# Attention scores of a two-layer kernel in tiles of four heads by 32 queries, over only the keys up to them

## The reference, cut to what matters

```python
q = (x @ Wq).reshape(B, S, 16, 192)            # 128 without, 64 with rotation
k = concat([k_nope, broadcast(k_rope)])        # k_nope, v from a 64-wide latent
scores = einsum('bqhd,bkhd->bhqk', q, k) / sqrt(192)
scores = where(tril(ones((S, S))), scores, finfo.min)
attn = softmax(scores, axis=-1)
out = einsum('bhqk,bkhd->bqhd', attn, v).reshape(B, S, 16 * 128) @ Wo
```

## Time and profile before

| | |
|---|---|
| time, median of 3 runs | 873.41 us (871.42 to 873.88) |
| profiled execution | 871.95 us, span of its instructions 870.2 us |
| PE busy | 831.8 us (96%) |
| DVE, ACT, POOL busy | 715.8 (82%), 543.4 (62%), 478.7 us (55%) |
| mean granted PE clock | 0.988 |

### The profile page before, as it was taken

The page is one execution under the profiler, slowest core; times in us unless marked ns, Lnnn a source line. Parts: engine busy times, 40 slices in busy tenths (PEclk is TensorE's granted clock), DMA queues, the critical chain, the costliest instruction groups (busy, mean ns, idle before and its releaser), DMA issues.

```text
span 870.2 us, 22877 instructions
## 1 busy us (share of the span) xinstructions
PE 831.8 (96%) x7736; PEld 759.5 (87%) x7736; DVE 715.8 (82%) x2467; ACT 543.4 (62%) x1611; POOL 478.7 (55%) x1245
## 2 busy tenths in 40 slices
PE   4989999999998789999999999999999999999996
PEld 3978999888897779999999999999999999999975
DVE  6898787898685768988889898898988989888874
ACT  5544444444655747677676676766777677786672
POOL 7832012113134655767657677575766757676653
PEclk9989999999999989999999999999999999999999
DMA  8510110000001111111111112121121111212110
GB/s 299 208 32 1 61 61 2 1 1 1 1 28 43 34 37 46 42 49 35 52 38 51 46 37 55 34 54 45 37 55 31 51 48 41 51 33 54 47 32 20
DMA packets 56277, 41.21 MB, mean 47 GB/s; under 512 B 30304, under 2 KB 53216, under 8 KB 55520
## 3 DMA queue, kind: packets, MB, share of 16 engines
q1 hardware_dynamic: 55968, 39.62, 16.2%
q10 hardware_dynamic: 192, 0.13, 0.1%
HBM read 14.53 MB, written 4.19 MB: 22 GB/s over the span
## 4 chain that ended last, share of the span: by engine, by line
PE 79%; SPq 7%; DVE 4%; POOL 4%; issue 3%; DMA 1%; ACT 1%; POOLq 0%; DVEq 0%; ACTq 0%
PE bank L472 49%; PE bank L660 16%; PE bank L686 8%; SPq L437 5%; SPq L368 3%; PE bank L534 2%; POOL par L1686 1%; PE bank L625 1%; PE bank L544 1%; DVE PT L1494 1%; DVE SM L1474 1%; DMA QT<-qa 1%; POOL G L1686 1%; PE bank L584 1%; PE bank L487 1%
## 5 line engine op out<-in xcount | busy, mean ns | idle before, releaser
L950 ACT ACTIVATE SM<-SM,stb 128x256 f32<-128x256 f32 (+1 forms) x512 | 226.5, 444 | 88.0 <-DVE stb L1474 87.1
L1858 POOL TENSOR_SCALAR SM<-SM,stb 128x256 f32<-128x256 f32 (+1 forms) x512 | 210.9, 430 | 117.3 <-DVE stb L1482 112.9
L660 PE MATMUL bank<-KT,QT 128*128 128x256 f32 (+1 forms) x1024 | 197.2, 333 | 10.4 <-DMA QT<-qa 5.2
L660 PEld LDWEIGHTS bank<-KT,QT 128*128 128x128 f32 x1024 | 150.1, 192 | 32.3 <-DVE stb L1474 10.4
L1474 DVE CUSTOM_DVE_ANT_0 SM<-bank,CONST 128x256 f32<-128x256 f32 (+1 forms) x512 | 154.7, 348 | 17.4 <-PE bank L660 16.0
L472 PE MATMUL bank<-yh,wq_lo 128*128 128x256 f32 x512 | 158.3, 309 | 0.0
L472 PE MATMUL bank<-yl,wq_hi 128*128 128x256 f32 x512 | 145.7, 285 | 0.0
L472 PE MATMUL bank<-yh,wq_hi 128*128 128x256 f32 x512 | 145.6, 284 | 0.0
L1494 DVE STREAM_TRANSPOSE PT<-SM 128x512 f32<-128x512 f32 x192 | 134.7, 702 | 9.0 <-PE bank L686 8.8
L472 PEld LDWEIGHTS bank<-yh,wq_lo 128*128 128x128 f32 x512 | 98.3, 192 | 1.6
L472 PEld LDWEIGHTS bank<-yl,wq_hi 128*128 128x128 f32 x512 | 98.1, 192 | 1.6
(11 more groups left out here) (204 smaller groups left out, 1957.0 us busy)
## 6 DMA issues: line engine op xcount, KB each, us to landing
QT<-qa SPq DMA_DIRECT2D x508, 32.0 KB, 1.9
C<-KV SPq DMA_DIRECT2D x256, 16.0 KB, 1.8
out<-fo SPq DMA_DIRECT2D x32, 128.0 KB, 1.8
X<-in_x SPq DMA_DIRECT2D x7, 512.0 KB, 11.1
stage<-in_wqn SPq DMA_DIRECT2D x2, 1024.0 KB, 9.6
stage<-in_wo SPq DMA_DIRECT2D x2, 1024.0 KB, 5.1
stage<-in_w1t SPq DMA_DIRECT2D x4, 256.0 KB, 5.5
stage<-in_w2t SPq DMA_DIRECT2D x2, 512.0 KB, 7.2
```

Of the source, the lines that this page charges most:

```text
L660: i = e.matmul(sbank[n % 2][:, nk * j:nk * j + nk], Q[:, h % 8, 128 * qt:128 * qt + 128], KT[b % 3][:, h % 2, 0:nk], start=True, stop=True)
L950: i = e.activation(M[:, nk * j:nk * j + nk], M[:, nk * j:nk * j + nk], ACT.Exp, bias=S[:, 0, j:j + 1], scale=-1.0, accum_out=S[:, 1, j:j + 1])
L1858: i = e.tensor_scalar(P[:, nk * j:nk * j + nk], P[:, nk * j:nk * j + nk], S[:, 2, j:j + 1], 1.0, ALU.mult, ALU.mult)
```

## The change

A unit of scores becomes a set of tiles of four heads by 32 queries, each over only the 32(q+1) keys up to the end of its query block q (0 to 7). There are ten units a batch, in a new order: for each half of the heads, two units of the blocks 6 and 7, two of the blocks 4, 5, 0, 1, one of the blocks 2 and 3 of both sets of four heads. The stationary operand holds 32 queries of four heads. To take it as one row of 128 equally spaced words, each head's queries are stored in QT and qa by place in block: token 32n + i at word 8i + n. So it is read with a step of eight words, and `queries` and `turn_queries` write with a step of eight words. `turn_queries` is two instructions instead of one. `most`, `exps` and `normalise` have widths of 32(q+1). `turn_weights` has two instructions in the units of four tiles. In `l1_pv` all heads' products of a query block skip the key blocks past it, so their width is 256, 192, 128 or 64. POOL clears the five SM buffers once after layer 0 (`clean`). Tokens are in natural order, so the reversals in `scan` and in POOL's tables go. All tables and lags were made anew for ten units, and some steps of layer 0 moved by one or two; with them units of scores stand behind `l1_pv` and `l1_q` of the same step instead of ahead of them.

```diff
-ORDER = (3, 0, 2, 1, 5, 4)
-UNITS = 12
+ORDER = (2, 3, 0, 4, 1, 7, 8, 9, 5, 6)
+UNITS = 10
-LAG_T, LAG_V, LAG_L = 4, 5, 6
-LAG_O, LAG_R, LAG_C = (8, 9), (8, 9), (9, 10)
+LAG_T, LAG_V, LAG_L = 4, 6, 6
+LAG_O, LAG_R, LAG_C = (7, 7), (8, 8), (9, 11)
-Q_AT = {2: (1, 0), 5: (3, 2), 9: (7,), 10: (5,), 11: (6, 4)}
+Q_AT = {0: (0,), 2: (1,), 3: (3,), 4: (2,), 6: (7, 5), 9: (6, 4)}
...
 def unit(n):
...
+    b, (h, k) = n // UNITS, divmod(ORDER[n % UNITS], 5)
+    if k < 2:
+        return b, h, [(k, 6, 0), (k, 7, 256)]
+    if k < 4:
+        return b, h, [(k - 2, 4, 0), (k - 2, 5, 192), (k - 2, 0, 384), (k - 2, 1, 448)]
+    return b, h, [(0, 2, 0), (0, 3, 128), (1, 2, 256), (1, 3, 384)]
+def tiles(n):
+    return [(p, q, slice(at, at + 32 * q + 32)) for p, q, at in unit(n)[2]]
...
+        def by_place(t):
+            return t.rearrange("p h (q n) -> p h n q", n=8)
...
             def l1_s(n):
...
-                for j, h in enumerate(hd):
-                    i = e.matmul(sbank[n % 2][:, nk * j:nk * j + nk], Q[:, h % 8, 128 * qt:128 * qt + 128],
-                                 KT[b % 3][:, h % 2, 0:nk], start=True, stop=True)
+                for p, q, at in tiles(n):
+                    i = e.matmul(sbank[n % 2][:, at], Q[:, 4 * p:4 * p + 4, :].rearrange("p h t -> p (h t)")[:, q::8], KT[b % 3][:, p, 0:32 * q + 32],
+                                 start=True, stop=True)
...
             def l1_pv(b, parts, units):
...
+                for qt, q0, q1 in parts:
+                    for kb in range(4 * qt + q1):
+                        q = max(q0, kb - 4 * qt)
+                        for i in range(4):
...
+                            for half in range(2):
+                                j = e.matmul(sums[64 * half:64 * half + 64, :, 128 * qt + 32 * q:128 * qt + 32 * q1],
+                                             C[rows_, kb, :], PT[qt][rows_, 2 * half:2 * half + 2, kb, q:q1, :],
...
             def queries(b, u):
...
-                e.activation(Q[0:64, h0:h0 + 4:2, :], src[0:64, :, :], ACT.Copy)
+                e.activation(Q[0:64, h0:h0 + 2, :, :], src[0:64, :, :, :], ACT.Copy)
...
             def turn_queries(b, g):
...
-                e.tensor_tensor(qa[r % 2][:, :, :, :], src.unsqueeze(1).broadcast_to([128, 2, 2, T]),
-                                TR[:, :, :].unsqueeze(2).broadcast_to([128, 2, 2, T]),
-                                ALU.mult).then_inc(SEM["qa"], 1)
+                for part in range(2):
+                    i = e.tensor_tensor(by_place(qa[r % 2][:, part, :, :]), src, TR[:, part, :].rearrange(
+                        "p (n q) -> p n q", n=8).unsqueeze(1).broadcast_to([128, 2, 8, 32]), ALU.mult)
+                i.then_inc(SEM["qa"], 1)
...
             def turn_weights(n):
...
+                for p, q, at in pairs[::2]:
+                    k = q + 2
+                    src = SM[n % 5][:, at:at + 64 * k].rearrange("p (q k c) -> p q k c", q=2, c=32)
+                    dst = PT[q // 4][:, 2 * h + p, 0:k, q % 4:q % 4 + 2, :].rearrange("p k q c -> p q k c")
+                    i = e.transpose(dst, src)
...
+            def clean():
+                after_mlp(w)
+                for i in range(5):
+                    e.memset(SM[i][:, :], 0.0).then_inc(SEM["clean"], 1)
```

More of the change, by code:

```diff
@@ L100, in shared_bank_order @@
         b, m = n // UNITS, n % UNITS
+        if m in MISC_AT and b + 2 < NB:
+            js.append(("mi", 2 * (b + 2) + MISC_AT.index(m)))
+        if (d := summed(n, LAG_V, 0)) is not None:
+            if len(js) % 2:
+                js.append(("pad", len(js)))
+            js += [("v", 4 * d + i) for i in range(4)]
         if m == LORA_AT and b + 1 < NB:
@@ L776, in _ @@
                 b, m = n // UNITS, n % UNITS
-                if n < TOTAL:
-                    l1_s(n)
+                if m in MISC_AT and b + 2 < NB:
+                    i = 2 * (b + 2) + MISC_AT.index(m)
+                    free_shared("mi", i)
+                    l1_misc(b + 2, i % 2, jof("mi", i))
+                for qt in range(2):
+                    if (d := summed(n, LAG_V, qt)) is not None and (qt or d == NB - 1):
+                        if d < NB - 1:
+                            l1_pv(d, ALL_PARTS, UNITS)
+                        else:
+                            l1_pv(d, LAST_PARTS if qt else FIRST_PARTS, UNITS if qt else FIRST_DONE)
                 if m == LORA_AT and b + 1 < NB:
@@ L801, in _ @@
                     l1_tk(b + 1, jof("tk", b + 1))
-                if n == UNITS * (NB - 1) + 5 + LAG_V:
-                    l1_pv(NB - 1, FIRST_PART, 6, counted=False)
-                for qt in range(2):
-                    if (d := summed(n, LAG_V, qt)) is not None and (qt or d == NB - 1):
-                        if d < NB - 1:
-                            l1_pv(d, ALL_PARTS, UNITS)
-                        elif qt == 0:
-                            l1_pv(d, MIDDLE_PART, 8)
-                        else:
-                            l1_pv(d, LAST_PART, UNITS)
         @block.scalar
@@ L945, in exps @@
             def exps(n):
[L946 to L947 removed]
+                M, S = SM[n % 5], st_b[n % 4]
                 w.wait_ge("mx", n + 1)
[L949 to L951 removed]
+                for j, (_, _, at) in enumerate(tiles(n)):
+                    i = e.activation(M[:, at], M[:, at], ACT.Exp, bias=S[:, 0, j:j + 1], scale=-1.0,
+                                     accum_out=S[:, 1, j:j + 1])
                 i.then_inc(SEM["p"], 1)
@@ L1946, in _ @@
                 b, m = n // UNITS, n % UNITS
-                for qt in range(2):
-                    if (d := summed(n, LAG_C[qt])) is not None:
-                        residual(2 * d + qt)
                 if m == KV_AT and b + 1 < NB:
@@ L2016 @@
     rope = wq[:, :, 128:]
+    heads = np.arange(NH).reshape(2, 2, 4).transpose(1, 0, 2).reshape(-1)
     wkva = a["L1_attn_Wkv_a"]
```

421 lines of the change are left out of this document (181 added, 240 removed).

## The result

The changed kernel takes 957.99 us (median of 4 runs, 956.74 to 959.55); the kernel before takes 872.41 in the same comparison. The ratio is 1.0986, with an interval of 1.0952 to 1.1021: it is slower by 10%. The forecast was 939 us with 920 to 960 as its own range.

The account below looks back on a forecast made before the run. PE's instruction stream was taken to bound layer 1; 16 x (+3.8 scores + 0.3 latent sums) + 0.5 for entry and end = +66 us on 871.95, giving 938, a median of 939.5; likeliest 939, own range 920 to 960.

Parts of the forecast that it names:

- The scores' loads: PE's score passes: eight-word-step loads cost twice the floor, 0.222 us a pass, making scores +3.8 us a batch; chance 0.37.
- The multiplier: Layer 1 on PE: the added time per batch, +3.8 + 0.3 us, was charged 16 times.
- Entry and end: Layer 0 and the ends: waits and extra DMA issues, together taken as +0.5 us once.
- Columns and the floor: PE's scores: a quarter fewer columns, only an eighth less time, 1.3 us a batch; loads set 0.111 us for narrow passes.
- Rival 1: Steps free everywhere on loads and writes: period 35.86 us, median 858 us (850 to 864); chance 0.29.
- Latent sums: PE's latent sums: 24 rounds in place of 18, equal columns, 0.3 us more a batch, at best 0.
- DVE's widths: DVE: minimum 1.6 us less a batch at 1.02 ns a column, transposes 1.1 less; worth nothing beside PE.
- Writes: Stepped writes taken as doubled: DVE gains 4.9 us a batch, ACT 4.7; both below PE's period, so costed at nothing.
- Rival 2: PE's load free, writes not: DVE becomes the bound, period 37.2 us, 878 us (860 to 907); chance 0.18.
- Rival 3: PE's scores: stepped loads cost three times the floor, 0.334 us a pass, +10.9 us a batch; chance 0.16.

Follow-up runs that it names:

- kernel 8: The kernel before, with only the scores' loads taking every eighth word: 946.84 us, ratio 1.084 to the kernel before.
- kernel 2: The changed kernel with its stepped load kept but adjacent writes in queries and turn_queries: 938.58 us, ratio 1.0773 to the kernel before.
- kernel 1: The changed kernel with adjacent loads and adjacent writes, no steps: 856.67 us, ratio 0.9824 to the kernel before.
- kernel 3: The changed kernel with its stepped writes kept but adjacent loads: 935.08 us, ratio 1.0739 to the kernel before.
- kernel 6: As kernel 1, but turn_queries on DVE writes with the step of eight words: 866.89 us, ratio 0.9932 to the kernel before.
- kernel 7: As kernel 1, but queries on ACT writes with the step of eight words: 919.79 us, ratio 1.0548 to the kernel before.
- kernel 12: As kernel 7, but query block 0 is issued two units later, beside block 1: 875.64 us, ratio 1.0037 to the kernel before.
- kernel 5: The changed kernel with QT stored by block, so loads are adjacent and ACT writes runs of 32 words: 861.42 us, ratio 0.9865 to the kernel before.
- kernel 9: As kernel 7, but exps moved ahead of queries in each step of ACT: 980.39 us, ratio 1.1231 to the kernel before.

## Why the prediction was right, and where it was off

**The scores' loads: the mechanism right, the term too small.** The forecast was 0.222 us a pass from a load that costs twice the floor. A pass costs about 0.235 from start to start (0.227 to 0.241 as the mean of a unit of eight, 0.238 in kernel 8 at 128 and at 256 columns); the records went from 190 to 335 ns as foretold ("over 300"). 64 x 0.013 is 0.8 us a batch. Kernel 2, with the stepped load alone, has a period of 41.83 us, where the sum gave 36.86 + 3.8 + 0.3 = 40.96.

**The multiplier: 16 where it should have been 13.** Kernel 2 nevertheless took 938.58 us against 939 forecast. I had charged each of 16 batches with the full change of the period. The thirteen periods between the marks carry it (13 x 4.97 = 64.6 us), but the rest of the span, three batches' worth, grew by only 2.1 us (936.9 - 543.8 = 393.1, against 870.2 - 479.2 = 391.0), not by 3 x 4.1 + 0.5 = 12.8. Entry and end have waits beside PE's work, which may have taken up the difference; no run shows that. The forecast of 939 left out what the writes cost, so it is kernel 2 that it describes, and it met kernel 2 by luck: the periods came out 11 us longer than forecast, entry and end 11 us shorter.

**Columns and the floor: right.** In kernel 1 passes of up to 128 columns took 0.111 us, those of 160 to 256 took 0.135, 0.163, 0.189 and 0.216; the forecast had 0.111, 0.134, 0.161, 0.188 and 0.215. A quarter of the columns went and an eighth of the time. Rival 1's sum, a period of 35.86 and 858 us, met 35.82 and 856.67: it is what the change is worth without its steps.

**Latent sums: right in size.** 192 passes take 4.35 us where 144 took 4.14, +0.2 against +0.3.

**DVE's widths: right.** The minimum of 256 columns takes 420 ns and that of 32 takes 186 in after:

```profile
L1463 DVE CUSTOM_DVE_ANT_0 SM<-bank,CONST 128x256 f32<-128x256 f32 x43 | 18.0, 420 | 0.0
L1463 DVE CUSTOM_DVE_ANT_0 SM<-bank,CONST 128x32 f32<-128x32 f32 x42 | 7.8, 186 | 0.0
```

(420 - 186)/224 is 1.04 ns a column, against the 1.02 that the saving was worked out with. DVE's busy time in a batch is 32.08 us, where it was 31.88, because the stepped writes took the saving back.

**Writes: the price nearly right, what it does to the time wrong.** "Doubled" was taken. ACT's copies went from 584 to 1124 ns, and ACT's batch to 29.36 us (forecast 29.7). For DVE it was too much: eight halves of 1130 in place of 682 ns are 3.6 us a batch, not 4.9, and DVE's batch is 32.08 us, not 34.1. But the step "Both stay below a PE period of 35.9, and far below one of 41", from which the writes were costed at nothing, failed. They cost 957.99 - 938.58 = 19.4 us beside the stepped load: 13 x 0.9 = 12 in the periods, of which the wait of PE's `l1_pv` for PT is 0.8, and 7 at the entry and the end. That is the term that turned 939 into 958, 2 us inside the forecast's own range.

**Rival 2: a real case, priced 57 us too low, with the wrong engine.** It gave 878 for free loads with doubled writes; kernel 3 took 935.08. I had looked at DVE, its 87% and its wait for PT. That alone is kernel 6, 866.89. What I left out was ACT, because 29.7 of 35.9 us looked safe. Its period of 41.1 is 35.8 plus 2.5 of waiting for the minimum, 1.2 more of waiting for PT, and 1.4 because the latent sums take some 5.75 us at a fallen clock, in all 40.9. I knew what each engine had to do in a batch and not in which order; kernels 7 and 12 show that the order set most of the price.

**Rival 3: a slip.** Its estimate of 1037 doesn't come out of its own 0.32 us a pass, which gives 1040. Nothing else hangs on it.

**The balance.** The spans differ by 85.9 us where I had 66.1. The periods account for 13 x (5.89 - 4.1) = +23.3, from the load's price (0.9 a batch) and the writes (0.9); entry and end for 9.3 - 12.8 = -3.5.

**What stays open.** How the 101 us of both steps split where they overlap. Why the clock fell after the waits in kernels 3 and 7 but not after the shorter ones of after, and in kernel 7 not after all of them: no run varied that alone. Where the 19 us come from that ACT's stepped copies cost in either order when they are apart. Kernel 1 and kernel 5 with the table of kernel 12 weren't tried. That ACT's order is the cause rests on kernel 12, which moved one block, and on the trace of kernel 7; kernel 9, meant to show it, showed another wait.

## What to carry to other kernels

Before a layout is changed, look at the innermost step of every operand that reads or writes it: up to two float32 words it was nearly free on PE's loads, ACT and DVE, and from four on it made a load 1.6 to 2 times as long and a write 1.6 to 1.9 times. Put the cut into the DMAs instead, where eight runs of 128 bytes in place of 1 KB cost DMA share and at most the 5 us between kernels 1 and 5. Narrower tiles bring only what the load floor leaves. And when an engine off the bound gets slower instructions, don't compare its busy sum with the period: follow its queue in order, and see what short work stands behind the slow one and who waits for that.

## What the runs showed of the hardware that I had not expected

- The price of a step is nearly flat from four words (330 ns a load) to sixteen (314), with 372 at twelve, and three words already cost about 260.
- The price of a stepped stationary load hides behind a wide pass, up to its length: in kernel 8 passes of 256 columns cost 0.238 us, hardly over the 0.215 of before, and those of 128 columns went from 0.111 to the same 0.238.
- The stepped load and the stepped writes don't add: 82 and 78 us alone, 101 together.
- A wait of 2.5 us of PE could cost another 2.9 us behind it, through the granted clock (0.60 in the latent sums of kernel 7 at 521 us), or nothing: one batch earlier, after the same waits, the clock was 1.00.
